# Every engine's operations from the last three pairs to the last slot in a new written-out sequence (linear attention, top-1 expert layer, one core)

## The reference

```python
h = _ln(x, ln_w, ln_b)
q, k, v = h @ Wq, h @ Wk, h @ Wv              # 16 heads; keys of 4, values of 8
gk = log_sigmoid(h @ gk_w1 @ gk_w2 + gk_b2) / 16
S = exp(g_t) * S + k_t v_t ;  o_t = q_t S       # a scan over the 256 positions
o = _rms(o, rms_w) * (g * sigmoid(g))           # g = h @ Wg
x = x + o @ Wo
x = x + gelu(_ln(x) @ W1 + b1) @ W2 + b2
x = _layernorm(x0 + x)
# then 8 experts, of which one row survives per token
scores = softmax(x @ gate_w + gate_b);  top 2 of 8 are chosen
for i in range(8):
    h = relu(x * w_i @ w1[i] + b1[i]);  y = h @ w2[i] + b2[i]
    out = where(w_i > 0, y, out)                # the later expert wins
x = _layernorm(x + out)
```

## Time and profile before

| what | value |
| --- | --- |
| time, median of 3 runs | 450.14 us (448.68 to 451.42) |
| the profiled execution: time, span | 452.75 us, 451.0 us |
| mean granted TensorE clock | 0.965 |
| busy: PE, DVE, ACT, POOL | 405.0, 369.5, 344.5, 326.8 us |

### The profile page before, as it was taken

One profiled execution on the slowest core, in us unless ns is written; L12 is line 12 of the kernel. 1 busy time (PEld: TensorE's weight loads), 2 busy tenths in 40 slices (PEclk: granted clock), 3 DMA queues, 4 the chain that ended last, 5 costly groups with the idle time before them and its releaser, 6 DMA issues.

```text
span 451.0 us, 10568 instructions
## 1 busy us (share of the span) xinstructions
PE 405.0 (90%) x2806; PEld 316.7 (70%) x2806; DVE 369.5 (82%) x1216; ACT 344.5 (76%) x980; POOL 326.8 (72%) x299
## 2 busy tenths in 40 slices
PE   5998999899889888999969999788999999999993
PEld 3554555555555555477849768678899999999993
DVE  6379999999999998647875888888777877778874
ACT  2576999999888995998786689467876777777772
POOL 2057799999999997585065556777777887777775
PEclk9999999999999998899996999689999999999997
DMA  7065675765766444070001116356686877776710
GB/s 221 9 164 140 153 175 124 182 155 131 173 141 150 118 121 113 2 233 2 0 25 45 40 41 240 107 149 179 195 261 199 241 204 197 201 208 194 205 59 21
DMA packets 44378, 62.20 MB, mean 138 GB/s; under 512 B 6670, under 2 KB 29713, under 8 KB 42400
## 3 DMA queue, kind: packets, MB, share of 16 engines
q1 hardware_dynamic: 39712, 52.20, 44.9%
q0 software_dynamic: 4320, 8.93, 5.3%
q10 hardware_dynamic: 288, 0.41, 0.3%
HBM read 47.99 MB, written 13.97 MB: 137 GB/s over the span
## 4 chain that ended last, share of the span: by engine, by line
POOL 33%; PE 33%; issue 16%; DVE 10%; ACT 5%; DMA 2%; POOLq 1%; ACTq 0%; DVEq 0%
POOL states L2168 17%; PE bank L761 11%; PE bank L745 10%; POOL o_scale L2180 4%; POOL x_sb L2186 3%; PE bank L395 3%; POOL out_rows L942 3%; POOL row_buffers L2159 3%; POOL slab L2174 2%; PE bank L408 1%; ACT row_buffers L461 1%; PE bank L751 1%; PE bank L384 1%; DVE st L485 1%; PE bank L1129 1%
## 5 line engine op out<-in xcount | busy, mean ns | idle before, releaser
L596 POOL DMA_INDIRECT expert_regions<-row_buffers,row_i x64 | 62.1, 971 | 50.1 <-DVE row_i L580 22.6
L942 POOL DMA_INDIRECT out_rows<-h2t x71 | 70.7, 995 | 30.4 <-issue 24.3
L761 PE MATMUL bank<-ew,h2t 128*128 x568 | 79.1, 283 | 4.6 <-DVE h2t L893 3.2
L2168 POOL TENSOR_TENSOR states<-states,queries 128x1024 f32<-128x1024 f32 x32 | 75.1, 2370 | 7.2 <-DVE states L1906 7.2
L745 PE MATMUL bank<-h2t,slab 128*128 128x128 f32 x568 | 78.4, 282 | 0.5 <-ACT h2t L779 0.5
L761 PEld LDWEIGHTS bank<-ew,h2t 128*128 128x128 f32 x568 | 69.5, 193 | 7.6 <-issue 6.0
L1906 DVE TENSOR_TENSOR_SCAN states<-bank,kv 128x512 f32<-128x512 f32 x64 | 72.9, 1200 | 0.6 <-ACT bank L1443 0.6
L745 PEld LDWEIGHTS bank<-h2t,slab 128*128 128x128 f32 x568 | 70.7, 196 | 1.3 <-issue 0.8
L786 ACT ACTIVATE h2t<-bank,slab 128x128 f32<-128x128 f32 x142 | 43.9, 364 | 9.9 <-PE bank L745 9.9
L884 DVE TENSOR_SCALAR h2t<-bank,slab 128x128 f32<-128x128 f32 x142 | 42.6, 341 | 1.1 <-PE bank L745 0.7
L779 ACT ACTIVATE h2t<-bank 128x128 f32<-128x128 f32 x71 | 19.6, 277 | 26.8 <-PE bank L751 25.2
(11 more groups left out here) (216 smaller groups left out, 925.1 us busy)
## 6 DMA issues: line engine op xcount, KB each, us to landing
slab<-in_slabs SPq DMA_DIRECT2D x71, 258.0 KB
kv<-values_by_head SPq DMA_DIRECT2D x30, 512.0 KB, 6.0
h2t<-expert_regions SPq DMA_DIRECT2D x71, 72.0 KB
x_sb<-in_x SPq DMA_DIRECT2D x32, 128.0 KB, 6.0
values_by_head<-row_buffers SPq DMA_DIRECT2D x15, 256.0 KB, 2.1
out_rows<-h2t POOLq DMA_INDIRECT x71
expert_regions<-row_buffers,row_i POOLq DMA_INDIRECT x64
expert_regions<-pad_record SPq DMA_DIRECT2D x9, 72.0 KB, 3.0
```

Of the source, the lines that this page charges most:

```text
L596: pool.indirect_dma_start(out=regions, out_offset=bass.IndirectOffsetOnAxis(ap=row_i[:, q, g:g + 1].bitcast(U32), axis=0), in_=rec[:, ring ...
L761: ins = pe.matmul(bank[7][:, 0:D], c_ht[:, s, c * P:(c + 1) * P], ew2[:, bass.ds(e * HC + c * D, D)], start=(c == 0), stop=(c == HC - 1 an ...
L942: pool.indirect_dma_start(out=out, out_offset=bass.IndirectOffsetOnAxis(ap=rc[:, q, D + 1:D + 2].bitcast(U32), axis=0), in_=c_y[:, item % ...
L2168: pool.tensor_tensor(half, half, queries[:, s, :].unsqueeze(1).to_broadcast([P, VL, T]), ALU.mult).then_inc(q_applied, 1)
```

## The change

The calls behind the attention loop are written in another order on PE, ACT, DVE and POOL, and the loops over `expert_step` and over `item` are written out to the last slot. Each engine has the same calls as before, 19 table loads on ACT among them; no function, wait or buffer is changed, and SP's list is the same. A few lines of the diff, on POOL:

```diff
             scatter(5, 5, 6)
+            store(11)
             scatter(5, 6, 7)
             scatter(5, 7, 8)
-            store(10)
-            store(11)
+            bias_rows_in(24)
+            bias_rows_in(25)
+            bias_rows_in(26)
             store(12)
```

More of the change, by code:

```diff
@@ L1357, in _ @@
             hidden(22)
+            back(21)
             turn(24)
-            back(21)
             hidden(23)
             back(22)
-            for k in range(27, STEPS_C):
-                expert_step(k)
+            hidden(24)
+            turn(25)
+            back(23)
+            hidden(25)
+            turn(26)
+            back(24)
+            hidden(26)
+            turn(27)
+            back(25)
+            hidden(27)
+            turn(28)
+            back(26)
+            hidden(28)
@@ new lines, in _ @@
+            hidden(36)
+            turn(37)
+            back(35)
+            hidden(37)
+            turn(38)
+            back(36)
+            hidden(38)
+            turn(39)
+            back(37)
+            hidden(39)
+            turn(40)
+            back(38)
+            hidden(40)
+            turn(41)
+            back(39)
+            hidden(41)
+            turn(42)
+            back(40)
+            hidden(42)
+            turn(43)
+            back(41)
+            hidden(43)
@@ new lines, in _ @@
+            hidden(51)
+            turn(52)
+            back(50)
+            hidden(52)
+            turn(53)
+            back(51)
+            hidden(53)
+            turn(54)
+            back(52)
+            hidden(54)
+            turn(55)
+            back(53)
+            hidden(55)
+            turn(56)
+            back(54)
+            hidden(56)
+            turn(57)
+            back(55)
+            hidden(57)
+            turn(58)
+            back(56)
+            hidden(58)
@@ L1365, in _ @@
+            hidden(66)
+            turn(67)
+            back(65)
+            hidden(67)
+            turn(68)
+            back(66)
+            hidden(68)
+            turn(69)
+            back(67)
+            hidden(69)
+            turn(70)
+            back(68)
+            hidden(70)
+            back(69)
+            back(70)
         @block.scalar
@@ L2154, in _ @@
+            relu(70)
+            norm_out(67)
+            rows_out(69)
+            norm_out(68)
+            norm_out(69)
+            rows_out(70)
+            norm_out(70)
         @block.gpsimd
@@ L2330 @@
+            store(65)
+            store(66)
+            bias_rows_in(69)
+            bias_rows_in(70)
+            store(67)
+            store(68)
+            store(69)
+            store(70)
 def kernel(**inputs):
```

892 lines of the change are left out of this document (682 added, 210 removed).

## The result

The changed kernel takes 447.0 us (median of 11 runs; the kernel before, beside it, 451.2, median of 11). The ratio is 0.9913, 95% interval 0.9896 to 0.9929: faster by 0.9%, or 3.9 us. One of the eleven executions took 780.31 us; the ratio leaves it out. The profiled execution took 446.81 us with a span of 445.0, 6.0 us less than the profiled execution of before. Those two numbers don't agree, and the first rows say why.

What follows compares the result with a forecast made beforehand. POOL's scatter chain, with waits for ACT's rows, was taken to set `hidden(24)`, with a fixed PE-bound stretch behind. 4.6 us there plus 0.5 at the end make 5.1; 450.14 - 5.1 = 445.0 us, range 442 to 447.9.

Steps and rivals of the forecast that it cites:

- The cause in phase B: Before slot 0, POOL's `sum_x(15)` beside DVE's L539 delays PE, which then runs at half clock; ACT's longest wait, 5.1 us.
- 1.6 us for DVE: Phase B: what DVE loses on L539 beside `sum_x(15)`, 1.91 us against 0.30; if kept, the gain is that much smaller.
- Phase B's size: Up to `scatter(2,0)`: fewer ACT waits, 3.0 us kept, bring it to 259.5 us, 7.4 us earlier.
- the rival of a larger gain: ACT hardly waits in phase B and later rows are never late: 8.9 + 0.5 us, 440.7 us; chance 0.20.
- the give-back: Slot 0 to the last scatter: late rows and two more stores on POOL cut the 7.4 us gain to 2.1.
- the colder PE: Rival: waits of PE near slot 0 lead to half clock, costing some 3.5 us: 448.5 us, no change; chance 0.20.
- Slot 24: Last scatter to `hidden(24)`: 5.0 us to `weigh(24)`, then the weigh and 2.2 us; `hidden(24)` at 344.2, 4.6 us earlier.
- PE would be there by 333: Slots 0 to 23: at 2.1 us a slot from 280.7 us PE reaches slot 24 by 333, so no limit.
- The end: Last two stores: `norm_out(69)` ahead of `rows_out(70)` makes the last some 0.5 us earlier, 0 to 0.9, if POOL is free.
- POOL's backlog: From slot 24 on: POOL idles about 5 us with some ten stores due; pairs of bias and store hide this by 3 us.
- The slower rival: Phase B keeps ACT's 11.2 us of waits while the slots' new order costs: `hidden(24)` 3.6 us later, 453.2 us; chance 0.12.
- a narrower rule: Phase B: a GpSimd instruction and a VectorE instruction using both its SBUF ports hold each other up; 1.6 us at stake.

Runs made afterwards that it cites:

- e4: The kernel before with only `sum_x(15)` moved ahead of the first scatter: 446.54 us, ratio 0.9902.
- e11: The kernel before with `sum_x(15)` two scatters later, behind the fourth, POOL's queue as long as before: 448.47 us, ratio 0.9955.
- e5: The changed kernel with `sum_x(15)` put back behind the second scatter: 450.82 us, ratio 0.9993 against the kernel before.
- e6: The changed kernel with ACT's row groups of batches 3 to 5 and DVE's `shift_of(5)` earlier: 448.36 us, ratio 0.995 against the kernel before.
- e3: The changed kernel up to slot 23, then the old fixed sequence, stores 12 to 20 ahead of the first bias: 448.44 us, ratio 0.995 against before.
- e12: The changed kernel with `store(10)` and `store(11)` moved behind the last scatter: 445.6 us, ratio 0.9882 against the kernel before.
- e1: The changed kernel's order up to the first turn of slot 0, then the order of the kernel before: 443.23 us, ratio 0.9827.
- e9: e1 with ACT's last three row groups and `shift_of(5)` earlier, all scatters ahead of stores, biases mixed in early: 446.07 us, ratio 0.9906 against before.
- e2: The old order up to slot 0, then the new one, `norm_rows(3,4,8)` kept ahead of `weigh(0)`: 455.32 us, ratio 1.0109 against the kernel before.
- e10: e1 with the first bias behind `store(12)` in place of `store(20)`, stores and biases mixed from there: 442.79 us, ratio 0.9807 against before.
- e7: The changed kernel with POOL's order alone altered, all scatters ahead of all stores: 451.84 us, ratio 1.0009 against the kernel before.

## Why the prediction was right, point by point

The forecast was 445.0 us, and 447.0 was measured, inside its own range of 442 to 447.9. The sign and the mechanism held; the gain forecast was 5.1 us and came to 3.9 by the runs, 2.9 by the two profiled executions. Of the 2.0 us between 445.0 and 447.0, 1.1 lie in the kernel before: its median is 451.2 over 11 runs, where the forecast started from 450.14.

**The cause in phase B was right.** L539 beside `sum_x(15)` made PE wait and run at half clock, and that was ACT's longest wait. e4 shows it by one move, e11 by keeping POOL's queue as it was. The forecast took it for one of several causes; by e4 the move of `sum_x(15)` is the main one: alone it brings 4.4 us. Put back behind the second scatter it takes all the gain away (e5), there with the longer queue as a second way. The forecast's 1.6 us for DVE left out L500, held by the other half.

**Phase B's size was right, the last of it by luck.** ACT was to wait 3.0 us from `evacuate(1)` on and waits 3.5, 2.8 of them for `transpose_rows`. `norm_rows(1,4,8)` was to end at 249.4 and ends at 245.12, 248.1 with the 3.0 us, so 1.3 us sooner than said. But `scatter(2,0)` then waits 1.47 us, 0.3 of it issue, for the landing of an earlier scatter, a wait that the forecast did not have. The two cancel: `scatter(2,0)` gains 7.3 us where 7.4 was said. Read straight from the two profiles it would be 10.3, as the rival of a larger gain had it: 3.0 of those belong to the execution of before.

**The terms that fail are those of the give-back.** `norm_rows(3,4,8)` was to end 3.7 us behind the start of `weigh(0)` and ends 4.6 behind (281.70), so `scatter(3,4)` gains 4.4 in place of 5.0. From there 53.7 us pass to the end of the last scatter where 52.2 were said. The work is as counted (50.9 us); 1.3 us of waits were allowed, and the two shown above (2.12 and 1.48, less 0.3 of issue each) are 3.0. The larger one was on no list: `store(1)`, now among the scatters, waits for DVE's `norm_out(1)`, which stands behind 4.5 us of `slot_table(1,0)` and `slot_table(1,1)`. e6 shows the same kind of wait grow to 4.18 us where ACT is made to serve the scatters first. The smaller one comes of PE's clock, as the paragraph on the colder PE shows. In e3 and e5, where `scatter(5,0)` does not wait, the same way takes 52.5 and 52.3 us. So of 7.3 us nothing is left at the last scatter of this execution, where 2.1 were expected; with the way as long as in e3 and e5 some 1.3 would be. e12 and e1 agree: two stores fewer, or the old order, move the last scatter forward.

**Slot 24 had more to spare than said:** 4.15 us from the last scatter's end to `weigh(24)`, where 5.0 was taken, then 3.0 to `hidden(24)`, where 2.6 was. That gave 2.9 us for the 2.5 forecast. That PE would be there by 333 was too early: in e9, where PE waits 1.0 us from 306 to 338, `hidden(24)` starts 61.6 us behind `weigh(0)`, 2.6 us a slot and not 2.1. The sum did not rest on it.

**The end was to bring 0.5 us and brings nothing:** from `hidden(24)` to the last store's start it is 99.41 us, and was 99.40. POOL's backlog was not as well hidden as said: DVE waits 2.8 us for biases at two slots, but the stretch from `hidden(24)` to `hidden(70)` is only 0.3 us longer (92.14 us for 91.87). e9 shows what it costs at the very end.

**The colder PE came, later than said, and cost about 1.2 us of the profiled execution.** In slots 0 to 23 PE is busy 57.67 us at a clock of 0.89, before 53.83 at 0.93. PE waits 1.76 us behind `slot_table(1,0)` and (1,1), and from 301.0 to 307.8 us its granted clock is 0.51. In e5, whose lists are the same there, the same wait stands and the clock stays at 1.00. PE's group of products behind that wait and the later relu of ACT that waits for PE, after the change:

```profile
301.14 2.07 PE L761 MATMUL bank<-ew,h2t 128*128 x8 [1.76 <-DVE h2t L893]
```

```profile
307.87 0.63 ACT L786 ACTIVATE h2t<-bank,slab 128x128 f32<-128x128 f32 x2 [2.30 <-PE bank L745]
```

The same two in e5, and its `scatter(5,0)`:

```profile
305.44 1.15 PE L761 MATMUL bank<-ew,h2t 128*128 x8 [1.76 <-DVE h2t L893]
```

```profile
309.42 0.63 ACT L786 ACTIVATE h2t<-bank,slab 128x128 f32<-128x128 f32 x2 [0.52 <-PE bank L745]
```

```profile
319.92 0.96 POOL L596 DMA_INDIRECT expert_regions<-row_buffers,row_i  x1 [0.30 <-issue]
```

`norm_rows(5,0,4)`, which stands behind that relu and later ones, comes 37.2 us behind `weigh(0)` after the change and 34.3 in e5, and `scatter(5,0)` waits 1.48 us for it in the one and not at all in the other. ACT's 3.81 us of waiting for the records of slot 24 hide the later slots, but not this. How often the runs of the changed kernel have such a fall is not known.

**The slower rival** named a cost that is there: where phase B brings nothing, the slots' order costs 4.9 us (e2), where 3.1 were said. In the whole change phase B paid for it.

## What to carry to other kernels

Before a new order of whole lists is judged, look for the one collision that it removes: here one call of POOL moved by two places gives as much as the change, and of the rest of the new order the part up to slot 0 is worth keeping (e1), with an early first bias at most (e10). An operation that feeds a later stage (scatters, rows) is moved ahead of the running stage only until something else bounds it; past that point each place moved turns up as a wait elsewhere (`store(0)` in e6, slot 20 in e7, the last store in e9). And two profiles are put on a common mark in a stretch that both share before their times are subtracted.

## What the runs showed of the hardware

The collision of DVE and POOL is a lock, and not a slower rate. In e11 L549 ends at 233.71 us, as POOL's first half ends (233.67), and L552 at 235.07, as the second ends (235.04): 1.68 and 1.12 us for operations that take 0.16 and 0.17 in e4. L551 between them takes its 0.17 us; it starts as the second half does (233.74), so it doesn't show what happens to an operation with one tensor in. In e5 it is L558 that ends (235.61) where POOL's first half does (235.48). The prediction weighed a narrower rule. The Trainium skill (SBUF — State Buffer, SBUF: two separate sides) says that a DVE instruction with two inputs from SBUF shares a port pair with a POOL instruction that reads SBUF, and that the later of the two waits for the whole of the other. The trace agrees as far as it goes: the operations that are held (L539, L549, L552, L558, and L500 before) have two tensors from SBUF, and each ends within 0.13 us of POOL's. But in three of the first four DVE's record starts 0.25 to 0.5 us ahead of POOL's, and DVE is held all the same; a start as the record gives it does not tell who holds the port.

An operation with one tensor in can be held as well. `norm_out` (L909, from SBUF to SBUF) takes 0.34 us in most places; after the change it takes 1.63 us beside a run of bias adds on POOL and ends at 423.12, as the third of them does (423.03). Before, it takes 0.52 us beside a store of POOL and ends at 446.04, as the making of that store does (445.98), while L549 in e4 takes its 0.16 us beside a scatter.

```profile
421.49 1.63 DVE L909 TENSOR_SCALAR h2t<-h2t 128x128 f32<-128x128 f32 x1
```

`sum_x(15)` in its new place runs from 207.79 to 210.41 us, and DVE's operations beside it (adds with one input from PSUM, statistics) keep their usual 0.69 and 0.87 us. So the price of a collision is set by which operations fall together, and here moving by 20 us left none to be seen.

One more: two executions of the same lists differed by 3.0 us at 190 us, and what differs between them is PE's pace (0.91 and 1.00 of the clock granted from 160 to 200 us, and slower products in the first 17 us). What decides it is open; the fall at 301 us, which e5 does not have behind the same wait, is of the same kind.
